# Attention outputs turned by VectorE in 32x32 blocks instead of by TensorE and ScalarE, small norm steps moved to GpSimd

## The reference, cut to what matters

```python
q, k = rope(rms_norm(q, wq), rms_norm(k, wk))
o1 = softmax(q @ k.T * 0.25 + causal) @ v          # self, 16 heads
x1 = layernorm(x + o1 @ w_proj.T)
o2 = softmax(Q @ K.T / 4 + causal + mask) @ V      # cross, 16 heads
x2 = layernorm(x1 + o2 @ Wo)
h  = rmsnorm(x2, gamma) ; g = gelu(h @ w1.T + b1)  # heavy and light
x3 = layernorm(x2 + g @ w2.T + b2)
```

## Time and profile before

| | |
|---|---|
| runs | 992.27, 995.03, 995.65 us, median 995.03 |
| the profiled execution | 991.54 us, span 989.8 us from first to last instruction |
| busy share of the span | PE 91%, PEld 71%, DVE 74%, ACT 50%, POOL 50% |
| mean granted TensorE clock | 0.966 of full speed |

### The profile page before, as it was taken

One profiled execution on the slowest core, in us unless ns is written; L12 is line 12 of the kernel. 1 busy time (PEld: TensorE's weight loads), 2 busy tenths in 40 slices (PEclk: granted clock), 3 DMA queues, 4 the chain that ended last, 5 costly groups with the idle time before them and its releaser, 6 DMA issues.

```text
span 989.8 us, 21917 instructions
## 1 busy us (share of the span) xinstructions
PE 903.1 (91%) x7904; PEld 707.7 (71%) x7904; DVE 731.6 (74%) x1842; ACT 495.7 (50%) x1063; POOL 498.5 (50%) x905
## 2 busy tenths in 40 slices
PE   3367888999999999999999999999999999898886
PEld 2335565787878787787878787877878787776676
DVE  7777678677878878877878788887777788574612
ACT  1132443646465555646475655546464655446342
POOL 6454464545555564645464655646455555243221
PEclk8669899999999999999999999999999999999998
DMA  3884091936657290927566381918465572804000
GB/s 108 122 167 67 20 134 22 125 38 98 77 65 109 39 135 10 130 39 108 67 87 88 49 125 25 129 25 120 54 95 81 66 97 37 127 3 76 13 1 22
DMA packets 79644, 74.24 MB, mean 75 GB/s; under 512 B 8592, under 2 KB 78896, under 8 KB 79536
## 3 DMA queue, kind: packets, MB, share of 16 engines
q1 hardware_dynamic: 75008, 68.11, 48.9%
q10 hardware_dynamic: 4528, 4.73, 1.9%
HBM read 17.49 MB, written 4.20 MB: 22 GB/s over the span
## 4 chain that ended last, share of the span: by engine, by line
PE 55%; DVE 20%; issue 8%; DMA 7%; SPq 4%; POOL 3%; ACT 2%; ACTq 0%; POOLq 0%; DVEq 0%
PE bank L359 52%; DVE mx L931 9%; DMA stk1k<-nat1k 4%; SPq L282 4%; POOL pr L1249 2%; PE bank L386 2%; DVE qn L1064 2%; ACT pr L763 1%; PE bank L585 1%; DVE x L1012 1%; DMA stk2k<-nat1k 1%; POOL rstd L1239 1%; DVE nat2q L914 1%; DVE nat2q L916 1%; DVE rest L907 1%
## 5 line engine op out<-in xcount | busy, mean ns | idle before, releaser
L763 ACT ACTIVATE pr<-bank 128x384 f32<-128x384 f32 x512 | 241.1, 502 | 194.3 <-PE bank L359 194.0
L931 DVE TENSOR_REDUCE mx<-bank 128x3 f32<-128x384 f32 x512 | 264.3, 550 | 81.8 <-PE bank L359 80.1
L1249 POOL TENSOR_SCALAR_AFFINE_SELECT pr<-pr 128x256 f32<-128x256 f32 x512 | 226.7, 454 | 184.5 <-ACT pr L763 181.6
L359 PE MATMUL bank<-cmaskb,idb 128*128 128x256 bf16 x512 | 144.4, 282 | 32.9 <-DMA stk2k<-nat1k 13.9
L359 PE MATMUL bank<-w,g 128*128 128x256 f32 x576 | 170.8, 389 | 1.1 <-ACT g L775 1.1
L775 ACT ACTIVATE g<-bank,b 128x256 f32<-128x256 f32 x144 | 68.2, 474 | 91.6 <-PE bank L359 91.3
L1273 POOL TENSOR_TENSOR xTlow<-xT,xThigh 128x512 fp32r<-128x512 f32 x16 | 20.7, 1297 | 149.4 <-ACT xThigh L699 149.4
L359 PEld LDWEIGHTS bank<-w,g 128*128 128x128 f32 x576 | 89.6, 190 | 5.2 <-ACT g L775 1.5
L359 PEld LDWEIGHTS bank<-cmaskb,idb 128*128 128x128 bf16 x512 | 50.2, 98 | 59.5 <-DVE mx L931 28.7
L359 PE MATMUL bank<-stk2k,stk2q 97*128 97x128 bf16 (+1 forms) x512 | 85.1, 253 | 0.0
L359 PE MATMUL bank<-stk1k,stk1q 97*128 97x128 bf16 (+1 forms) x512 | 82.3, 248 | 0.0
(11 more groups left out here) (159 smaller groups left out, 1870.8 us busy)
## 6 DMA issues: line engine op xcount, KB each, us to landing
stk1q<-nat1q SPq DMA_DIRECT2D x90, 128.0 KB, 4.3
stk1k<-nat1k SPq DMA_DIRECT2D x90, 128.0 KB, 6.6
stk2k<-nat2k SPq DMA_DIRECT2D x90, 128.0 KB, 4.5
stk2q<-nat2q SPq DMA_DIRECT2D x90, 128.0 KB, 6.0
xT<-in_xT SPq DMA_DIRECT2D x16, 256.0 KB, 7.6
ctxT<-in_ctxT SPq DMA_DIRECT2D x16, 256.0 KB, 7.7
x<-in_x SPq DMA_DIRECT2D x16, 256.0 KB, 6.2
out_x<-x SPq DMA_DIRECT2D x16, 256.0 KB, 5.8
```

The costliest lines, as they stand in the source:

```text
L359: return nc.tensor.matmul(out, lhsT, rhs, start=start, stop=stop, skip_group_check=check)
L763: nc.scalar.activation(pr[:, h % (2 * HG), :], ring_bank("T", a, b, h)[:, 0:3 * P], ACT.Exp, scale=HD ** -0.5)\
L931: V.tensor_reduce(mx3[:, h, :], scored[:, 0:3 * P].rearrange("p (k t) -> p k t", k=3), AX.X, ALU.max, negate=True).then_inc(s_mx[a], 1)
L1249: G.affine_select(out=slot, in_=slot, compare_op=ALU.is_ge, fill=0.0, base=0, pattern=[[0, 2], [1, P]], channel_multiplier=-1).then_inc(s_ ...
```

## The change

ScalarE's copies of the value groups (`copy_group`, `copy_out`) and PE's transposes (`out_tokens`, `out_dims`) are gone. VectorE reads each group straight from its bank with a transpose of 32x32 blocks (`blocks`), so that tokens lie on partitions within each block; for two groups at a time it divides and turns the blocks back (`normalise_pair`) into `onT`, which the projection reads. The rows of the projection's weights are permuted on the host to fit (`by_blocks`). The variance plus epsilon of all three norms, the small arithmetic of the rms norm, and layer norm 3 (of all batches but the last) move from VectorE to GpSimd. SP issues the store of the output behind the two loads of the row maxima instead of ahead of them.

```diff
-                copy(oT[:, gr, :], bank[OT_BANK][:, 0:T]).then_inc(s_oT[a], 1)
...
+            def blocks(a, b, gr):
+                n = C * b + gr // PG + 1
+                dve.wait_ge(s_pv[a], NG * b + gr + 1)
...
+                V.transpose(tok[:, gr, :], bank[OT_BANK][:, 0:T]).then_inc(s_tok[a], 1)
+            def normalise_pair(a, b, pair):
+                n = C * b + pair + 1
+                groups = slice(PG * pair, PG * (pair + 1))
+                dve.wait_ge(s_tok[a], NG * b + PG * (pair + 1))
+                o = tok[:, groups, :].rearrange("p g (k w) -> p g k w", w=VW)
+                V.reciprocal(rden[a][:, groups, :], o[:, :, :, HD]).then_inc(s_rd[a], 1)
+                dve.wait_ge(s_rd[a], n)
+                V.tensor_tensor(on[:, pair, :].rearrange("p (k g d) -> p g k d", g=PG, d=HD), o[:, :, :, 0:HD],
+                                rden[a][:, groups, :].rearrange("p g (k o) -> p g k o", o=1)
+                                .to_broadcast([P, PG, NB, HD]), ALU.mult).then_inc(s_on[a], 1)
+                dve.wait_ge(s_on[a], n)
+                wait(dve, s_o[a], b)
+                V.transpose(onT[a][:, pair, :], on[:, pair, :]).then_inc(s_onT[a], 1)
...
 def values(a, b, gr):
-                    pe.wait_ge(s_oT[a], NG * b + gr)
+                    pe.wait_ge(s_tok[a], NG * b + gr)
...
 VectorE, step(i):
+                if live(s):
+                    blocks(1, s, 0)
                 if live(f):
                     scale2(f)
                 if live(i + 1):
                     split(1, i + 1, 1, 1)
+                if live(s):
+                    blocks(1, s, 1)
...
                 if live(s):
+                    normalise_pair(1, s, 0)
+                    blocks(1, s, 2)
                     take_rest(2, s, 1, 0)
-                    normalise_heads(1, s)
+                    blocks(1, s, 3)
+                    normalise_pair(1, s, 1)
                     split_rest(2, s, 1, 0)
-                if live(l):
+                if l == B - 1:
                     layer_norm(3, l)
...
                     add_residual(1, s, PROJ_BANK[1], x0)
                     statistics(1, s)
+                if live(c):
+                    blocks(2, c, 0)
...
                     newton(i + 2, 1)
                     newton(i + 2, 2)
+                if live(c):
+                    blocks(2, c, 1)
+                    normalise_pair(2, c, 0)
...
+            def inverse_deviation(a, b):
+                pool.wait_ge(s_mv[a], TT * (b + 1))
+                wait(pool, s_rs[a], b)
+                G.tensor_scalar(ve[a][:, :], mv[a][:, :, 1], LN_EPS, None, ALU.add).then_inc(s_ve[a], 1)
+                power(rstd[a][:, :], ve[a][:, :], s_rs[a], s_ve[a], b)
...
 GpSimd, step(i), between x1c and the masks of T1:
+                if live(i - 4) and i - 4 < B - 1:
+                    layer_norm3(i - 4)
                 if live(f):
-                    power(rstd[2][:, :], ve[2][:, :], s_rs[2], s_ve[2], f)
+                    inverse_deviation(2, f)
+                    inverse_norm2(f)
...
-X1T_AT, OUT2_AT, Q2_AT = 1, (3, 5, 10, 12), 4
+X1T_AT, OUT2_AT, Q2_AT = 1, (3, 11), 4
-K2_AT, OUT1_AT, QK1_AT, V1_AT = 1, (3, 4, 8, 10), (3, 9), 13
+K2_AT, OUT1_AT, QK1_AT, V1_AT = 1, (3, 9), (3, 9), 13
```

## The result

| | before | after |
|---|---|---|
| median of the runs | 995.18 us (992.27 to 995.65, 4 runs) | 1149.6 us (1144.06 to 1154.54, 4 runs) |
| the profiled execution | 991.54 us, span 989.8 | 1153.53 us, span 1151.8 |
| mean granted TensorE clock | 0.966 | 0.901 |

The change makes the kernel slower: 1.1557 times the time of before, 95% interval 1.1488 to 1.1627. The forecast was 1119 us with a range of 1055 to 1175, slower at 93%; the time lies in the range, 31 us above the forecast.

The account below looks back on a forecast made before the run. PE was taken to set the pace, busy 54.4 of 55.0 us a turn. Transposes saved, four waits and clock summed to +9.3 us a full turn, +124 in all: 1115.5 profiled, 1119 us median, range 1055 to 1175.

Parts of the forecast that it names:

- The transposes on PE: PE loses 24 identity transposes a turn in the two attentions, 0.11 us each: -2.64 us a turn.
- first rival: VectorE empties the bank in time, so PE keeps the whole 2.64 us a turn: 953 us, chance 6%.
- Transposes on VectorE: Twelve block transposes of 128x256 a turn added on VectorE, taken at 0.42 us each like the division.
- Wait A: T2, before values 2.1: PE waits for the transpose behind squares, `roots_qk`, residual and statistics 1; 4.5 us a turn.
- Wait C: Before values 1.3: PE waits for self attention's third transpose, behind norm 3's statistics and the first pair; 1.85 us.
- D: Before values 2.0: PE waits for the mask of head 3, as PE's transposes no longer fill the time; 0.6 us.
- Wait B: T2, before values 2.2: PE waits for the transpose behind layer norm 1 and all Newton steps; 3.45 us a turn.
- the clock: PE at half clock behind its long waits, much of it falling into the next wait; 1.5 us a turn, ends 0 and 5.2.
- The rival with 5.2 us: PE's clock stays at half through S1's start, costing 5.2 us a turn instead of 1.5: 1167 us, chance 10%.
- done in time: S1, behind values 2.2: values 2.3 needs one transpose and one pair, finished in time, so no wait was counted.
- GpSimd delays T1: Rival: norm steps ahead of T1's masks on GpSimd cost as its dearest rows, +2.2 us a turn: 1148 us, chance 8%.
- What would show it: Signs: turn 62 to 66 us, PE busy under 54, waits over 4 before values 2.1 and over 3 before values 2.2.

Follow-up runs that it names:

- the fastest version: Against the run with the early squares: x1 transposes and values 2.3 ahead of S1's first head, cross attention's second pair ahead of S1's fourth maximum; 982.27 us.
- the run with filled waits: Changed kernel plus matmuls that nobody reads on PE, 36 ahead of values 2.1 and 26 ahead of values 2.2; 1123.18 us.
- the first experiment: Changed kernel with VectorE's transpose of values 2.0 moved ahead of `roots_qk` and that of values 2.1 behind Newton step 0; 1066.16 us.
- the run with the early squares: Changed kernel with three VectorE transposes moved earlier, query half 1 and its squares brought forward, layer norm 1 behind two Newton steps; 996.04 us.

## Why the prediction was right, and where it was off

**What bounds the kernel.** PE set the pace before: 24 more transposes a turn showed in the time. After the change no engine does in T2.

**The transposes on PE, -2.64 us a turn.** Doubling them cost 2.1, so the size holds within 0.5. The gain isn't to be had in T2 without more, though: that the 1.32 us there lie under the stack loads, the prediction did not see. It did not matter for the forecast, as T2 became longer, but its first rival, 953 us with all loops hidden, is not borne out: with the waits for `tok` gone the kernel took 996 us, and the fastest version 982.

**Transposes on VectorE, 0.42 us.** They take 0.437. The estimate of 0.62 by the Trainium skill's page "VectorE: DVE Perf Modes", "The three transpose paths", was too long; the division of the same shape was the right neighbour. VectorE is busy 45.79 us of the turn, 44.19 before.

**Wait A, 4.5 us.** It is 4.39, with the steps as named: squares, `roots_qk`, residual, statistics, transpose. Moving the one transpose ahead of `roots_qk` took A away, and moving the projection brought it to 2.60.

**Wait C, 1.85, and D, 0.6.** They are 1.71 and 0.63. (The steps that the prediction names for C add to 1.9.)

**Wait B, 3.45 us, and the clock, 1.5: the first of two terms that were mis-sized.** The wait itself is only 2.58, but from values 2.1 to values 2.2 it is 7.20 us (534.43 to 541.63), where the sum had 6.5. PE's own work in between, put at 3.06, took 7.20 - 2.58 = 4.62, as values 2.1 and the heads behind it ran at half clock, and the loop, which starts from those heads, closed 0.7 later: head 11 starts 1.44 us behind values 2.1 (534.43 to 535.87), where it was 0.79. With the waits filled and the clock at full, the same way takes 6.47 (521.24 to 527.71), so loop B was sized rightly and the 0.7 is the clock's. Then half clock went on into S1: 541.5 to 546.0 is at 0.66 with PE busy 4.37 of 4.5 us, which loses 0.34 x 4.5 = 1.5. Other turns differ: in the 4.8 us from values 2.2 on the granted clock lies between 0.50 and 1.00 over the thirteen full turns, a loss of 0 to 2.4, 1.4 in the mean. So the clock costs 0.7 + 1.5 = 2.2 us in this turn, not 1.5; the run with filled waits gives 2.0 in the mean. The prediction said that much of the lower clock would fall into the next wait; it was the clock behind the last wait, where none follows, that counted most. The rival with 5.2 us fell.

**S1, which I found "done in time": the second.** Values 2.3 was (no wait of it), but the maxima were not: PE waits for `mx` 12.0 us in 6.9 turns, 1.7 a turn, where before it was 3.2 in 8.4, 0.4. In this turn it is the 1.20 us of head 9 of S1, where before it was 0.23. Head 9 needs the bank that S1's seventh maximum reads, the first of these five on VectorE:

```profile
553.46 2.40 DVE L863 TENSOR_REDUCE mx<-bank 128x3 f32<-128x384 f32 x5
```

It begins 10.10 us behind the start of S1 (543.36), where before it was 9.50 (519.23 to 528.73). VectorE is at its first maximum sooner than before (0.78 us behind the start of S1 instead of 1.93), but then waits 1.33 us for a head of PE, and the second pair takes 1.6 us ahead of the sixth maximum, where two divisions took 1.24. PE, without its transposes there, is ready for head 9 0.4 us sooner. That is the term that the prediction put at nothing.

**The sum** for the turn: -2.64 + 4.39 + (7.20 - 3.06) + 1.71 + 0.63 + 1.5 + 1.20 = +10.9 of the measured 11.24 (66.24 - 55.0). As before had 0.2 to 0.4 of the last term, 0.5 to 0.7 is left unexplained; with the 2.1 that the doubling gives in place of 2.64, next to nothing is. The forecast had 9.3. Over all turns the difference is 66.6 - 55.0 = 11.6, times 13 is 151; the profiled executions differ by 162, so the ends cost about 11, not the 3 that I counted for turns 14 to 16 and the ends together. For turns 14 and 15 the terms that the prediction names add to 5.2 each, not 4; there A is 1.83 and 1.98, as forecast (1.8), and B 2.70 and 2.86 instead of 3.55. What else the ends hold is open. That the forecast missed the median by 31 us and not by 38 is chance: it was built on profiled executions (1115.5, measured 1153.53), and the profiled one lies 3.5 us under the median before and 3.9 above it after.

**GpSimd delays T1.** That rival fell: the small steps take 0.22 and 0.24 us, not a power's 0.71 (the variance step 0.22; I took 0.25), and PE waits for GpSimd's masks 2.9 us in 6.9 turns, never longer than 0.4. What the norm steps on GpSimd and the later store are worth by themselves, no run shows.

**What would show it.** The turn came out just above the 62 to 66 us; A, B and C lie where they were said to, B shorter than "over 3". That PE would be busy less than 54 us was wrong: 54.97, as matmuls at half clock count double.

## What to carry to other kernels

When a bank that was emptied by an idle engine is handed to one with a long ordered queue, price the queue, not the operation: 0.44 us of transpose cost 4.4 us of PE because of what stood ahead of it. Put what frees a shared buffer ahead of every step that waits for someone else, and before counting work taken off the pacing engine as a gain, look which transfer runs beside it and when it can start.

## What the runs showed of the hardware

- TensorE at half clock after waits: in the changed kernel the granted clock was 0.50 in the 1.5 us behind each of the thirteen waits of 4.4 us (values at 1.51 us instead of 0.86), and behind seven of the thirteen waits B. The length of the wait does not settle it: in the first experiment B is 2.25 us in each of thirteen turns, and the clock was 0.50 at once behind four of them and stayed at 1.00 for the next 5.5 us behind five; behind 1.70 us in the run with the early squares it was 0.53 (520.60 to 524.00), and behind the 1.71 us of C in the turn shown 1.00. What decides between them, no run here shows. Matmuls into an unused bank during the waits held the mean clock at 0.99 and saved 26 us of 1150.
- 128x128 float32 transposes on TensorE overlap: 0.11 us from one to the next, 0.09 by the time of the whole kernel, where the records give 273 ns each.
- A VectorE block transpose of 128x256 float32 takes 437 ns from PSUM, about as long as an elementwise pass of the same shape (0.42 us).
